# Degree count of a graph layer: the quotient one-hots stored with the chunk innermost, and one stair of every third group turned into a one-hot of VectorE

## The chip, the cores and the metric

One NeuronCore of one Trainium2 chip runs the kernel. The metric is the device time of one execution in microseconds (us), as the median of repeated runs.

## The reference

One layer of a graph network on 6,250 nodes of 512 features and 106,250 edges (50,000 drawn ones, both ways, and a loop for each node). Cut to what matters:

```
Q = relu(x @ Wq + bq);  V = x @ Wv + bv
deg  = segment_sum(ones, dst);  dinv = rsqrt(max(deg, 1e-12))
gcn  = segment_sum((x @ Wg)[src] * dinv[src] * dinv[dst], dst) + bg
out  = former(Q, V) + gcn + V          # cosine and sine sweeps over Q and V
out  = layernorm(x + relu(layernorm(out)))
```

The change lies in how `deg` is counted. Nothing else of the result is touched.

## The kernel before

The nodes are taken as 49 tiles of 128. The edges are sorted by `dst` and stand as 831 **chunks** of 128, one chunk in a column (a partition for each edge). The kernel has a first phase, in which for each tile t `x` is turned, multiplied by Wg and kept (`g_tile`), and a long second phase that gathers rows of `x @ Wg`, runs the sweeps and writes the output. The program of each engine is written out in order by hand, and the engines meet at semaphores.

The degree count rides on the first 31 tiles of the first phase (`HIST_TILES`). Each of these tiles does three **groups** b = 3t, 3t+1, 3t+2 of nine chunks (93 groups in all). `dst` is split into the remainder by 128 (`dst_mod`, the node in its tile) and the quotient (`dst_div`, the tile). For a group there are two operands in SBUF, each with two buffers that alternate:

- `div_hot`, the **quotient one-hots**: for each of the nine chunks 49 columns, 1 where the column's number is the edge's quotient. One VectorE instruction makes all 9 x 49 = 441 elements (L980), from the row 0..48 of `iota_bf`, read again for each chunk, and `dst_div`, of which one element is read 49 times.
- `mod_hot`, nine **wide hots** of 128 columns: for the first five chunks (`HOTS`) VectorE compares `iota_bf` with the remainder (a one-hot, L984, five instructions); for the last four (`STAIRS`) ScalarE takes the sign of column number plus 0.5 minus remainder (a stair of -1 and +1, L638, four instructions).

TensorE then multiplies, for each chunk, the wide hot by the quotient one-hots and adds into bank 5 (L1443, nine matmuls of 49 columns a group): one-hots into columns 0..48, stairs into columns 64..112. After tile 30 the stairs' sums are turned into counts by one small matmul.

The order of work in a tile t of the first 31:

- TensorE: wait for x's lower part of tile t; turn x of tile t+2 (L1428, four transposes); half of the product with Wg (L1382 to L1384, six matmuls of 512 columns); group 3t; the other half; groups 3t+1 and 3t+2.
- ScalarE: stairs of group 3t; copy turned x of t+2 from PSUM (L617, `g_step`); stairs of 3t+1 and 3t+2; copy the product of tile t (L621, `g_keep`); in tiles 0 to 7 one square of a kept tile (L626); in tiles 2 and 4 also a rounding of a weight (L602).
- VectorE: group 3t; lower part of x of tile t+2 (L993, `g_split`, waits for L617); groups 3t+1 and 3t+2; then what `between_tiles` puts there: a piece of a weight in odd tiles from 3 to 17 (L917), edge columns at tiles 6 and 8, limits of the tiles from 27 on.
- GpSimd fills constants at the start (`iota_bf` and others) and is idle until the second phase.

TensorE's group waits for VectorE (`bins_ready`) and ScalarE (`stairs_ready`); both wait for TensorE's group b-2 before they write into its buffer (`bins_used`).

Of the kernel before, what the change touches and what calls it, by code (L numbers as in the profile page):

```python
# [9 lines left out]
BF16 = mybir.dt.bfloat16  # L10
# [3 lines left out]
ALU = mybir.AluOpType  # L14
# [3 lines left out]
P = 128  # L18
# [12 lines left out]
def done(n):  # L31
    return n + (1 + LEAD)


def freed(n, depth):
    return n + (1 + LEAD - depth)


def build_layer(nc, x, src, dst, Wq, bq, Wv, bv, Wg, bg, gamma, beta, out):
# [3 lines left out]
    TILES = -(-N // P)  # L43
# [4 lines left out]
    GROUP, STAIRS = 9, 4  # L48
    HOTS = GROUP - STAIRS
# [5 lines left out]
    PAIRS = 4  # L55
# [30 lines left out]
    with ctx:  # L86
        def sb(name, shape, dt):
            return ctx.enter_context(nc.sbuf_tensor(name, shape, dt))
# [4 lines left out]
        def bank(name):  # L93
            return ctx.enter_context(nc.psum_tensor(name, [P, D], F32))
# [7 lines left out]
        pairs = sb("pairs", [P, PAIRS, PAIR], F32)  # L102
        with nc.sbuf_tensor("operands_f16", [P, 8, 2 * D], F16) as operands_f16:
# [40 lines left out]
        banks = [bank(f"bank{n}") for n in range(8)]  # L144
# [31 lines left out]
        dst_div = extra_row[:, :].bitcast(BF16)[:, 0:COLS]  # L176
# [3 lines left out]
        mod_hot = [hot_room[:, h * GROUP * 64:(h + 1) * GROUP * 64].bitcast(BF16).rearrange("p (c j) -> p c j", j=P)  # L180
                   for h in range(2)]
        DIVW = TILES + 1
        div_base = 2 * GROUP * 64
        div_hot = [hot_room[:, div_base + h * GROUP * DIVW // 2:div_base + (h + 1) * GROUP * DIVW // 2]
                   .bitcast(BF16).rearrange("p (c j) -> p c j", j=DIVW) for h in range(2)]
        iota_bf = sb("iota_bf", [P, P], BF16)
        zero_bf = sb("zero_bf", [P, P], BF16)
        UNIT_AT, STAIR_AT = 0, 64
# [46 lines left out]
        def column(ap, c):  # L235
            return ap[:, c:c + 1] if isinstance(c, int) else ap[:, bass.ds(c, 1)]
# [266 lines left out]
        def _(pool):  # L503
# [7 lines left out]
                               pattern=[[-1, P]], channel_multiplier=1).then_inc(s["consts_set"], 1)  # L511
            pool.iota(node_id[:, :], pattern=[[1, P]], base=0, channel_multiplier=0,
                      allow_small_or_imprecise_dtypes=True)
            pool.iota(iota_bf[:, :], pattern=[[1, P]], base=0, channel_multiplier=0,
                      allow_small_or_imprecise_dtypes=True)
            pool.iota(chunk_id, pattern=[[P, GROUPS]], base=0, channel_multiplier=1,
                      allow_small_or_imprecise_dtypes=True)
            pool.iota(first_node[:, :], pattern=[[P, TILES]], base=0, channel_multiplier=0,
                      allow_small_or_imprecise_dtypes=True)
# [8 lines left out]
                               pattern=[[-1, P]], channel_multiplier=1).then_inc(s["undo_ready"], 1)  # L528
            pool.wait_ge(s["undo_ready"], 2)
            pool.affine_select(out=undo, in_=undo, compare_op=ALU.not_equal, fill=-0.5, base=1,  # L530
                               pattern=[[-1, P]], channel_multiplier=1).then_inc(s["undo_ready"], 1)
            pool.wait_ge(s["undo_ready"], 3)
            pool.affine_select(out=undo[:, 0:1], in_=undo[:, 0:1], compare_op=ALU.not_equal, fill=0.5, base=1 - P,
                               pattern=[[-1, 1]], channel_multiplier=1).then_inc(s["undo_ready"], 1)
# [59 lines left out]
        def _(act):  # L594
# [39 lines left out]

            def stairs(b):
                act.wait_ge(s["bins_used"], freed(b, 2))
                for n in range(STAIRS):
                    last = act.activation(mod_hot[b % 2][:, HOTS + n, :], iota_bf[:, :], ACT.Sign,  # L638
                                          bias=column(stair_edge, b * STAIRS + n))
                last.then_inc(s["stairs_ready"], 1)  # L640
# [48 lines left out]
            for t in range(0, TILES):  # L689
                if t == 0:  # L690
                    act.wait_ge(s["columns_ready"], 1)
                if t < HIST_TILES:
                    stairs(3 * t)
                if t + 2 < TILES:
                    g_step(t + 2, t % 2, rows_of(t + 2))
                if t < HIST_TILES:
                    stairs(3 * t + 1)
                    stairs(3 * t + 2)
# [125 lines left out]
        def _(dve):  # L824
# [151 lines left out]
            def bins(b):  # L976
                c0, half = b * GROUP, b % 2

                dve.wait_ge(s["bins_used"], freed(b, 2))
                dve.tensor_tensor(div_hot[half][:, :, 0:TILES],  # L980
                                  iota_bf[:, 0:TILES].unsqueeze(1).to_broadcast([P, GROUP, TILES]),
                                  dst_div[:, c0:c0 + GROUP].unsqueeze(2).to_broadcast([P, GROUP, TILES]), ALU.is_equal)
                for c in range(HOTS):
                    last = dve.tensor_scalar(mod_hot[half][:, c, :], iota_bf[:, :], column(dst_mod, c0 + c), None,  # L984
                                             ALU.is_equal)
                last.then_inc(s["bins_ready"], 1)
# [72 lines left out]
            for t in range(0, TILES):  # L1059
                if t < HIST_TILES:  # L1060
                    bins(3 * t)
                keep_beside_g(t)
                if t + 2 < TILES:
                    g_split(t + 2, t % 2, rows_of(t + 2))
                if t < HIST_TILES:
                    bins(3 * t + 1)
                    bins(3 * t + 2)
                beside_g(t)
                between_tiles(t)
# [63 lines left out]
            h = stage[:, 2, 0:TILES]  # L1133
# [237 lines left out]
        def _(pe):  # L1371
# [65 lines left out]
            def bins(b):  # L1437
                half = b % 2
                pe.wait_ge(s["bins_ready"], done(b))
                pe.wait_ge(s["stairs_ready"], done(b))  # L1440
                for c in range(GROUP):
                    at = UNIT_AT if c < HOTS else STAIR_AT
                    last = pe.matmul(banks[5][:, at:at + TILES], mod_hot[half][:, c, :], div_hot[half][:, c, 0:TILES],  # L1443
                                     start=False, stop=False, skip_group_check=True)
                last.then_inc(s["bins_used"], 1)

# [20 lines left out]
            def g_tile(t, n, r):  # L1467
                pe.wait_ge(s["g_x_split"], done(t))
                if t + 2 < TILES:
                    g_turn(t + 2)  # L1470
                pe.wait_ge(s["g_kept"], freed(t, 2))
                g_product(t, n, r, [0, 1])
                if t < HIST_TILES:
                    bins(3 * t)
                g_product(t, n, r, [2, 3]).then_inc(s["g_summed"], 1)
                if t >= QV_TILES:
                    qv_beside_g(t)
                if t < HIST_TILES:
                    bins(3 * t + 1)
                    bins(3 * t + 2)  # L1480
                if t == HIST_TILES - 1:
                    pe.matmul(banks[5][:, 0:P], zero_bf[:, :], zero_bf[:, :], start=False, stop=True,
                              skip_group_check=True).then_inc(s["degrees_summed"], 1)
                between_tiles(t)
# [236 lines left out]
```

## Time and profile before

| what | value |
|---|---|
| runs of the kernel before | 1686.92 us median of 3 (1683.31 to 1688.21) |
| profiled execution | 1702.43 us, its span 1700.6 us |
| TensorE busy | 1529.1 us (90%) |
| VectorE busy | 1093.6 us (64%) |
| ScalarE busy | 608.9 us (36%) |
| GpSimd busy | 916.2 us (54%) |
| first and last quotient one-hots (L980) | start at 21.7 and 186.4 us |

The shares are means over the whole span. The degree count lies in its first 190 us; after that TensorE goes on with tiles 31 to 48 alone, and GpSimd's gathers begin at about 340 us. Starting times of an instruction are read as the pace of its engine, since the duration that the profile gives to one instruction overlaps with the next one's by some 80 ns on VectorE and ScalarE and more on TensorE.

### The profile page before, as it was taken

Reading aid. Unit: us, or ns where it says so; the run is one execution under the profiler, and the core shown is the slowest. Engines: PE = TensorE matmul, PEld = TensorE weight load, DVE = VectorE, ACT = ScalarE, POOL = GpSimd, SP = SyncE. Lnnn points to the kernel's source line nnn. Section 1 sums busy time; section 2 is a strip of 40 time slices with the busy share of each in tenths; the row PEclk is TensorE's granted clock in tenths of the full one; section 3 lists DMA queues with packets and bytes.
Section 4 is the critical chain, followed back from the end, with each engine's and each line's share of the span. In section 5 each row is a group of like instructions: output and inputs, shape, how many; then the busy total and the mean of one; then the engine's idle time right before and its main releaser. Section 6 shows DMA issues by size and latency. Waiting matters only on the chain.

```text
span 1700.6 us, 25340 instructions
## 1 busy us (share of the span) xinstructions
PE 1529.1 (90%) x7913; PEld 943.0 (55%) x7913; DVE 1093.6 (64%) x3318; ACT 608.9 (36%) x1384; POOL 916.2 (54%) x1026
## 2 busy tenths in 40 slices
PE   5788999899999997999998999889999999999994
PEld 3566777666555563443433433336666766666663
DVE  6999676676666666434445444447777768777774
ACT  5999875533233222111112111113333333333332
POOL 0000000166666766666676777666666666666662
PEclk9999999999999997999999999989999999999997
DMA  6444444598888888888888888879888888888884
GB/s 224 139 154 160 151 157 153 201 314 291 297 285 286 290 287 263 262 266 267 266 253 257 264 270 273 271 208 288 283 271 279 277 271 277 286 273 271 285 256 142
DMA packets 172759, 423.89 MB, mean 249 GB/s; under 512 B 24142, under 2 KB 25802, under 8 KB 172616
## 3 DMA queue, kind: packets, MB, share of 16 engines
q0 software_dynamic: 71120, 236.74, 45.5%
q1 hardware_dynamic: 79980, 146.16, 25.1%
q10 hardware_dynamic: 21516, 39.29, 6.1%
q8 instruction: 65, 1.06, 0.2%
q14 instruction: 78, 0.64, 0.1%
HBM read 351.42 MB, written 70.67 MB: 248 GB/s over the span
## 4 chain that ended last, share of the span: by engine, by line
PE 60%; issue 12%; DVE 10%; DMA 7%; POOL 4%; ACT 4%; another core or an unknown queue 1%; POOLq 0%; SPq 0%; DVEq 0%; ACTq 0%
PE bank L1382 13%; PE bank L1383 12%; PE bank L1384 12%; PE bank L1503 10%; PE bank L1505 9%; POOL gathered L566 4%; DMA gathered<-scaled_g,index_slots 3%; DVE stage L984 3%; DVE stage L980 2%; ACT stage L638 1%; DMA scaled_g<-pairs 1%; DVE operands L993 1%; ACT operands L617 1%; DMA combine<-values 1%
## 5 line engine op out<-in xcount | busy, mean ns | idle before, releaser
L566 POOL DMA_INDIRECT gathered<-scaled_g,index_slots x882 | 877.1, 994 | 418.1 <-issue 203.8
L1100 DVE TENSOR_SCALAR one_hot<-iota_bf,dst_in_tile,gathered 128x128 bf16<-128x128 bf16 x882 | 269.7, 327 | 373.8 <-DMA gathered<-scaled_g,index_slots 212.9
L1503 PE MATMUL bank<-gathered,one_hot 128*128 128x512 f16 x882 | 344.9, 391 | 77.0 <-issue 39.4
L1382 PE MATMUL bank<-weights,operands 128*128 128x512 f32 x784 | 398.4, 508 | 14.2 <-DVE stage L1000 4.4
L1505 PE MATMUL bank<-gathered,one_hot 128*128 128x512 f16 x882 | 339.6, 385 | 5.1 <-issue 4.6
L1383 PE MATMUL bank<-weights,operands 128*128 128x512 f32 x784 | 313.7, 400 | 1.8 <-issue 1.8
L1384 PE MATMUL bank<-weights,operands 128*128 128x512 f32 x784 | 312.6, 399 | 0.6 <-issue 0.6
L1503 PEld LDWEIGHTS bank<-gathered,one_hot 128*128 128x128 bf16 x882 | 85.5, 97 | 253.5 <-issue 163.5
L736 ACT ACTIVATE operands_f<-operands,cos_sin_v 128x512 f16<-128x512 f32 x98 | 70.2, 721 | 360.5 <-remote 171.2
L1382 PEld LDWEIGHTS bank<-weights,operands 128*128 128x128 f32 x784 | 150.7, 192 | 80.7 <-issue 7.6
L551 POOL COPY dst_slots<-dst_cols 128x18 f32 x49 | 12.7, 260 | 332.7 <-issue 331.2
L1384 PEld LDWEIGHTS bank<-weights,operands 128*128 128x128 f32 x784 | 149.4, 191 | 38.9 <-issue 2.3
L1383 PEld LDWEIGHTS bank<-weights,operands 128*128 128x128 f32 x784 | 150.8, 192 | 26.2 <-issue 3.9
L755 ACT ACTIVATE operands<-stage,stats 128x512 fp32r<-128x512 f32 x98 | 70.9, 723 | 228.4 <-issue 121.0
L1384 PE MATMUL bank<-operands_f,nodes 128*128 128x512 f16 x392 | 149.1, 380 | 3.9 <-issue 3.9
L1382 PE MATMUL bank<-operands_f,nodes 128*128 128x512 f16 x392 | 149.3, 381 | 1.3 <-issue 1.3
L1383 PE MATMUL bank<-operands_f,nodes 128*128 128x512 f16 x392 | 149.3, 381 | 0.5 <-issue 0.3
L638 ACT ACTIVATE stage<-iota_bf,combine 128x128 bf16<-128x128 bf16 x372 | 115.8, 391 | 8.1 <-DVE combine L873 6.3
L1505 PEld LDWEIGHTS bank<-gathered,one_hot 128*128 128x128 bf16 x882 | 87.7, 99 | 43.2 <-issue 7.5
L1382 PE MATMUL bank<-gathered,operands 128*128 128x512 f32 (+1 forms) x196 | 85.0, 434 | 0.0
L984 DVE TENSOR_SCALAR stage<-iota_bf,nodes 128x128 bf16<-128x128 bf16 x465 | 83.5, 247 | 0.0
L1189 DVE SCALAR_TENSOR_TENSOR operands_f<-operands,cos_sin_v,operands_f 128x512 f16<-128x512 f32 x98 | 73.0, 746 | 14.2 <-ACT operands_f L736 8.8
(243 smaller groups left out, 2066.8 us busy)
## 6 DMA issues: line engine op xcount, KB each, us to landing
operands<-values SPq DMA_DIRECT2D x98, 256.0 KB
stage<-in_x SPq DMA_DIRECT2D x96, 256.0 KB, 2.7
turned_x<-operands SPq DMA_DIRECT2D x37, 512.0 KB, 3.3
operands<-turned_x SPq DMA_DIRECT2D x37, 512.0 KB
gathered<-scaled_g,index_slots POOLq DMA_INDIRECT x882
scaled_g<-pairs SPq DMA_DIRECT2D x49, 260.0 KB, 2.0
pairs<-scaled_g SPq DMA_DIRECT2D x49, 260.0 KB
values<-stage ACTq DMA_DIRECT2D x49, 256.0 KB
```

Source lines behind the costliest of these rows:

```text
L566: pool.indirect_dma_start(out=plain(row_ring[k % RING]), out_offset=None, in_=table, in_offset=bass.IndirectOffsetOnAxis(ap=index_slots[:, ...
L638: last = act.activation(mod_hot[b % 2][:, HOTS + n, :], iota_bf[:, :], ACT.Sign, bias=column(stair_edge, b * STAIRS + n))
L736: act.activation(v_hi, m_values(g), ACT.Copy, scale=column(cos_sin_v, g % TILES * 2 + g // TILES))\
L755: act.activation(operands[:, 5 + n % 2, :], stage[:, 2 + j, :], ACT.Square, bias=st[:, 1:2], accum_out=st[:, 2:3]).then_inc(s[f"o_squared{ ...
L984: last = dve.tensor_scalar(mod_hot[half][:, c, :], iota_bf[:, :], column(dst_mod, c0 + c), None, ALU.is_equal)
L1100: dve.tensor_scalar(one_hot[:, k % HOT, :], iota_bf[:, :], column(dst_in_tile, seq % 2 * PER_TILE + k), scale_of(row), ALU.is_equal, ALU.m ...
L1189: dve.scalar_tensor_tensor(v_lo, m_values(g), column(cos_sin_v, g % TILES * 2 + g // TILES), v_hi, ALU.mult, ALU.subtract).then_inc(s["m_s ...
L1382: pe.matmul(out_ap, a_hi, b_hi, start=start and n == 0, stop=False, skip_group_check=True)
L1383: pe.matmul(out_ap, a_hi, b_lo, start=False, stop=False, skip_group_check=True)
L1384: last = pe.matmul(out_ap, a_lo, b_hi, start=False, stop=stop and n == len(pairs) - 1, skip_group_check=True)
L1503: pe.matmul(gcn_banks[seq % 2][:, :], one_hot[:, k % HOT, :], hi, start=k == 0, stop=False, skip_group_check=True)
L1505: pe.matmul(gcn_banks[seq % 2][:, :], one_hot[:, k % HOT, :], lo, start=False, stop=False, skip_group_check=True).then_inc(s["chunk_summed ...
```

## The change

The nine quotient one-hots of a group are stored with the chunk innermost: element (quotient j, chunk c) at 9j + c, where it was at 50c + j. VectorE makes them in one instruction as before; its first operand is now a new constant, `counter`, in which each number 0..49 stands nine times in a row (450 elements, made by GpSimd at the start, in room of `pairs` that is not used until much later), and its second is the row of the group's nine quotients, read again for each j. All three operands are 2 bytes wide and have a step of one element. TensorE reads the 49 columns of a chunk with a step of nine elements, 18 bytes, where it read them next to each other.

In each third group of a tile (b % 3 == 2) VectorE makes six wide one-hots instead of five, and ScalarE three stairs instead of four.

```
-                   .bitcast(BF16).rearrange("p (c j) -> p c j", j=DIVW) for h in range(2)]
+                   .bitcast(BF16).rearrange("p (j c) -> p j c", c=GROUP) for h in range(2)]
+        counter = pairs[:, PAIRS - 1, 0:GROUP * DIVW // 2].bitcast(BF16).rearrange("p (j c) -> p j c", c=GROUP)
+
+        def hots_of(b):
+            return HOTS + (b % 3 == 2)
...
+            pool.iota(counter, pattern=[[1, DIVW], [0, GROUP]], base=0, channel_multiplier=0,
+                      allow_small_or_imprecise_dtypes=True)
...
-                for n in range(STAIRS):
+                for n in range(hots_of(b) - HOTS, STAIRS):
...
-                dve.tensor_tensor(div_hot[half][:, :, 0:TILES],
-                                  iota_bf[:, 0:TILES].unsqueeze(1).to_broadcast([P, GROUP, TILES]),
-                                  dst_div[:, c0:c0 + GROUP].unsqueeze(2).to_broadcast([P, GROUP, TILES]), ALU.is_equal)
-                for c in range(HOTS):
+                dve.tensor_tensor(div_hot[half][:, 0:TILES, :], counter[:, 0:TILES, :],
+                                  dst_div[:, c0:c0 + GROUP].unsqueeze(1).to_broadcast([P, TILES, GROUP]), ALU.is_equal)
+                for c in range(hots_of(b)):
...
-                    at = UNIT_AT if c < HOTS else STAIR_AT
-                    last = pe.matmul(banks[5][:, at:at + TILES], mod_hot[half][:, c, :], div_hot[half][:, c, 0:TILES],
+                    at = UNIT_AT if c < hots_of(b) else STAIR_AT
+                    last = pe.matmul(banks[5][:, at:at + TILES], mod_hot[half][:, c, :], div_hot[half][:, 0:TILES, c],
```

On VectorE the instructions of tile 2 stand as follows in the program before (`stage` holds both kinds of hots, `extra_row` the quotients; the first row is the last of group 6):

```order
L984 TENSOR_SCALAR stage<-iota_bf,nodes 128x128 x5
L993 TENSOR_TENSOR operands<-bank1,operands 128x512
L980 TENSOR_TENSOR stage<-iota_bf,extra_row 128x9x49
L984 TENSOR_SCALAR stage<-iota_bf,nodes 128x128 x5
L980 TENSOR_TENSOR stage<-iota_bf,extra_row 128x9x49
L984 TENSOR_SCALAR stage<-iota_bf,nodes 128x128 x5
```

and so in the changed program, where line numbers are six or seven higher (`pairs` holds the counter):

```order
L990 TENSOR_SCALAR stage<-iota_bf,nodes 128x128 x5
L999 TENSOR_TENSOR operands<-bank1,operands 128x512
L987 TENSOR_TENSOR stage<-pairs,extra_row 128x441
L990 TENSOR_SCALAR stage<-iota_bf,nodes 128x128 x5
L987 TENSOR_TENSOR stage<-pairs,extra_row 128x441
L990 TENSOR_SCALAR stage<-iota_bf,nodes 128x128 x6
```

The order is the same; the quotient compare runs as one row of 441 elements instead of nine rows of 49, and the third group has one more wide one-hot.

On ScalarE a tile of the count without a square stands so before (L617 and L621 are the two copies from PSUM):

```order
L638 ACTIVATE stage<-iota_bf,combine 128x128 x4
L617 CAST operands<-bank 128x512
L638 ACTIVATE stage<-iota_bf,combine 128x128 x8
L621 COPY nodes<-bank 128x512
L638 ACTIVATE stage<-iota_bf,combine 128x128 x4
```

and so after the change:

```order
L645 ACTIVATE stage<-iota_bf,combine 128x128 x4
L624 CAST operands<-bank 128x512
L645 ACTIVATE stage<-iota_bf,combine 128x128 x7
L628 COPY nodes<-bank 128x512
L645 ACTIVATE stage<-iota_bf,combine 128x128 x4
```

The stair that is gone is one of the eight between the two copies.

## Rows read from the trace of the kernel before

**Rows 1.** Busy time of each engine in stretches (start and end in us).

```profile
core 0: us, PE busy (x) PEld busy (x) DVE busy (x) ACT busy (x) POOL busy (x), PEclk, DMA share, GB/s
32.00:64.00 32.00, 22.78 (x235) 16.73 (x234) 27.42 (x110) 31.81 (x90) 0.00 (x0) 1.00 0.41 141
88.00:190.00 102.00, 85.78 (x861) 64.64 (x858) 98.20 (x382) 92.03 (x274) 0.00 (x0) 1.00 0.43 150
```

**Rows 2.** Timeline of VectorE, one tile; columns: start, duration, instruction, idle before.

```profile
142.84 0.69 DVE L993 TENSOR_TENSOR operands<-bank,operands 128x512 fp32r<-128x512 f32 x1 [0.25 <-ACT operands L617]
143.45 0.61 DVE L980 TENSOR_TENSOR stage<-iota_bf,extra_row 128x441 bf16<-128x441 bf16 x1
...
144.79 0.61 DVE L980 TENSOR_TENSOR stage<-iota_bf,extra_row 128x441 bf16<-128x441 bf16 x1
...
147.80 0.69 DVE L993 TENSOR_TENSOR operands<-bank,operands 128x512 fp32r<-128x512 f32 x1 [0.25 <-ACT operands L617]
```

**Rows 3.** Timeline of TensorE in the tile behind it.

```profile
146.27 0.40 PE L1443 MATMUL bank<-stage 128*128 128x49 bf16 x9 [0.71 <-DVE stage L984]
146.51 0.63 PE L1428 MATMUL bank<-ident,stage 128*128 128x128 f32 x4
...
150.12 0.40 PE L1443 MATMUL bank<-stage 128*128 128x49 bf16 x9
```

**Rows 4.** Timeline of ScalarE there.

```profile
145.35 0.59 ACT L621 COPY nodes<-bank 128x512 f32<-128x512 f32 x1 [0.20 <-PE bank L1384]
145.84 1.27 ACT L638 ACTIVATE stage<-iota_bf,combine 128x128 bf16<-128x128 bf16 x4
147.18 0.59 ACT L617 CAST operands<-bank 128x512 fp32r<-128x512 f32 x1
...
150.31 0.59 ACT L621 COPY nodes<-bank 128x512 f32<-128x512 f32 x1 [0.20 <-PE bank L1384]
```

**Rows 5.** Timeline of ScalarE, tiles 5 and 6.

```profile
54.97 2.45 ACT L638 ACTIVATE stage<-iota_bf,combine 128x128 bf16<-128x128 bf16 x8
57.32 0.57 ACT L621 COPY nodes<-bank 128x512 f32<-128x512 f32 x1
57.92 0.63 ACT L626 ACTIVATE squares_out<-nodes 128x512 bf16<-128x512 f32 x1
...
62.59 0.59 ACT L621 COPY nodes<-bank 128x512 f32<-128x512 f32 x1
```

**Rows 6.** Timeline of VectorE: L993 in the lists of tiles 9, 19, 27, 29, 30.

```profile
77.03 0.68 DVE L993 TENSOR_TENSOR operands<-bank,operands 128x512 fp32r<-128x512 f32 x1
...
127.95 0.69 DVE L993 TENSOR_TENSOR operands<-bank,operands 128x512 fp32r<-128x512 f32 x1 [0.25 <-ACT operands L617]
...
167.66 0.69 DVE L993 TENSOR_TENSOR operands<-bank,operands 128x512 fp32r<-128x512 f32 x1 [0.25 <-ACT operands L617]
...
178.69 0.68 DVE L993 TENSOR_TENSOR operands<-bank,operands 128x512 fp32r<-128x512 f32 x1
...
184.43 0.68 DVE L993 TENSOR_TENSOR operands<-bank,operands 128x512 fp32r<-128x512 f32 x1
```

**Rows 7.** Groups of VectorE by line and shape, 0 to 200 us.

```profile
L980 DVE TENSOR_TENSOR stage<-iota_bf,extra_row 128x441 bf16<-128x441 bf16 x93 | 57.0, 613 | 1.4 <-PE bank L1443 1.3
...
L939 DVE TENSOR_TENSOR nodes<-nodes 128x896 f32<-128x896 f32 x1 | 1.1, 1082 | 0.0
...
L937 DVE TENSOR_SCALAR nodes<-nodes 128x896 f32<-128x896 f32 x1 | 0.6, 616 | 0.0
```

**Rows 8.** Timeline of TensorE in tile 0, at its slower pace.

```profile
24.82 0.60 PE L1443 MATMUL bank<-stage 128*128 128x49 bf16 x9
25.24 0.78 PE L1382 MATMUL bank<-gathered,operands 128*128 128x512 f32 x1
```

**Rows 9.** Timeline at the start.

```profile
2.68 0.18 POOL L518 IOTA first_node<- 128x49 f32 x1
...
4.79 0.63 DVE L856 CAST nodes<-nodes 128x896 f32<-128x896 int32 x1 [1.53 <-DMA nodes<-in_dst]
```

## The prediction

> **What bounds the kernel now.** The change lies in the first 190 us, so I first read the busy times by stretch, not the page's shares. Between 32 and 64 us ScalarE is busy 31.8 of 32 us; between 88 and 190 us VectorE is busy 98.2 of 102 us, with ScalarE at 92.0 and TensorE at 85.8 [rows 1]. No engine is far behind: what an edit frees on one meets the next soon. So I read the three timelines of one tile and follow who releases whom. (Starts of instructions give the pace; I call L993 of a tile the start of its lap on VectorE.)
>
> The **short loop**, tiles 19 to 26: L993 starts at 142.84, two groups follow, and TensorE's last group of the tile starts at 146.27, having waited 0.71 us for VectorE: 3.43 us [rows 2, 3]. TensorE needs 0.24 us for the nine matmuls, then turns x (146.51); ScalarE's copy L617 starts at 147.18 and the next L993 at 147.80, having waited 0.25 us for that copy [rows 2 to 4]. 3.43 + 0.24 + 0.67 + 0.62 = 4.96 us, the pace of these tiles. The group ahead of L993 is outside this loop (its cover is the 0.25 us).
>
> The **long loop** takes two tiles: TensorE from its last group (146.27) through turn, product, group and product until ScalarE's L621 starts at 150.31, 4.04 us [rows 3, 4]; L621 0.49; four stairs; L617 0.62 until L993; and VectorE's 3.43. The stairs stand 1.34 us long there (145.84 to 147.18), but eight of them in a row take 57.32 - 54.97 = 2.35 us, 0.294 each [rows 4, 5], so four need 1.17. Sum 9.75, or 4.88 a tile: only 0.08 below the short one.
>
> In tiles 1 to 7 ScalarE's own list is as tight. From L621 to L621 is 5.27 us with a square [rows 5]; twelve stairs (3.53), L621 (0.60 until the square starts) and the square with its tail (0.63) leave 0.51 for L617, about what a copy takes, so the engine has hardly a gap. And the long loop with a square (57.92 less the copy: 0.73) is 10.48, 5.24 a tile. VectorE's own list is 0.61 + 3 x 1.34 = 4.64 us a tile [rows 2]; in the odd tiles from 9 to 17 it has L917 as well, of the same shape as L993 (0.6), and is full. L993 goes from 77.03 to 127.95 in ten tiles, 10.18 a pair, so 5.22 in the odd ones and 4.96 in the even [rows 6]. Tiles 28 and 29 have a long extra each and take 5.74 (178.69 to 184.43) [rows 6].
>
> **What each edit costs.** *The compare.* 441 elements take 613 ns. The same kind of instruction on 896 elements takes 1082, so an element costs 469/455 = 1.03 ns, one a clock; L937, which reads one tensor, takes 616 for 896, 466 less, which is two elements a clock [rows 7]. No row has a two-tensor instruction on 2-byte operands with a step of one throughout. Bounds: nothing, or half of 441 x 1.03 = 0.23 us saved. I take 0.23: before, one operand repeats an element innermost, after the change all three run through neighbours, and the nearest row, L937, shows the engine at two a clock once it has the room. The Trainium skill (Vector Engine (DVE) Microarchitecture Reference, 5.1 Performance modes) states that two-tensor instructions run two elements a cycle when all are 2 bytes with an innermost step of one and more than one element, and that one element read repeatedly keeps them at one. It makes the same sum, and the 613 ns of before agree with its second half.
>
> *The sixth one-hot.* 1.34 us a group (143.45 to 144.79) less the compare's 0.53 leaves 0.81 for five, so 0.16 each on VectorE [rows 2]. In the stretch L993 to TensorE's last group both groups save 0.23 and the second gains 0.16: 0.30 less. VectorE's whole lap loses 3 x 0.23 - 0.16 = 0.53. *The third stair.* ScalarE's lap loses 0.29, all of it between L617 and L621, thus in neither loop; it counts only where ScalarE's list is the bound.
>
> *The strided read.* 837 matmuls read 49 elements 18 bytes apart. They start 0.24/9 = 27 ns apart now [rows 3]. No row has such a read. Below, nothing. Above, the nearest row is the same nine matmuls at TensorE's slower pace in tile 0: 25.24 - 24.82 = 0.42, 47 ns each, 20 more [rows 8]. I take 16 more, near that end, since the clock is granted in full there [rows 1], 49 columns at 2.4 GHz are 20.4 ns of the 27, and a column that costs two clocks makes 41 to 47. That is 0.144 us a group. It falls into the short loop once and the long loop twice, and half of what VectorE gave goes back. By the Trainium skill (Advanced Engine Details and Errata, SBUF Cachelines) a line is 16 bytes, and full speed wants two hits on one; 18 bytes never hit twice, so the rule speaks against this edit, but gives no figure. By the rule unheeded the sum is 9.9; with my value it is 6.6.
>
> *The counter.* An IOTA of 49 elements takes 0.18 us [rows 9]; 450 make under 1.7 at that rate even with nothing fixed, in front of what VectorE's constants wait for. VectorE waits there 1.53 us for the edges [rows 9] and later for a weight, so I cost it at nothing; without that cover it would be up to 1.7.
>
> **The sum.** New short loop 4.96 - 0.30 + 0.144 = 4.80; new long loop 9.75 - 0.30 + 0.288 = 9.74 for two tiles, 4.87; with a square 10.47.
> - Tiles 1 to 5: ScalarE's list is the bound (two weights are rounded there): 5 x 0.29 = 1.46. Tiles 6, 7: the long loop with a square hardly moves (10.48 to 10.47), so they add nothing; less 0.1 for tile 0's groups: 1.4.
> - Tiles 8 and 9: the first also turns the source columns and follows the short loop, 0.16; the second is VectorE's whole lap, 0.53: 0.7.
> - Tiles 9 to 18, five pairs after that: 10.18 becomes 9.74: 5 x 0.44 = 2.2.
> - Eight laps from 127.95 to 167.66 [rows 6]: 4.96 becomes 4.87: 0.75.
> - Tiles 27 to 30, VectorE's lap: 0.41, 0.53, 0.53, then 0.30 less 0.14 for the last: 1.6.
>
> Together 6.6 us. Behind the count TensorE is the bound and was waiting for its last group, so what it gains moves everything after it. The profiled execution would go from 1702.4 to 1695.8, and the median from 1686.9 to **1680.3**, 0.39% less; the profiled execution stands 15.5 us above the median, and I take the same gain off both. A measurement of this kernel can tell about 0.3%, 5.1 us, from no change.
>
> **Rivals.**
> - *The read is free.* Loops 4.66 and 9.45: tiles 1 to 7 1.8, tiles 8 and 9 0.8, five pairs 3.65, eight laps 1.9, the last 1.8: 9.9; 1677.0. For it: a matmul has 6.6 ns over its columns' time now, room in which a slower read could begin. Against: no row reads with a gap, so nothing shows it. 22%.
> - *TensorE becomes the bound, slower than before.* TensorE's own lap is 150.12 + 0.24 - 146.27 = 4.09 [rows 3]. Each ns on a matmul takes 0.009 us from each of some 25 tiles, 0.225 us; my 6.6 at 16 ns are gone at 45 ns more, that is 72 ns or more than three clocks a column. At 50 more its lap is 4.09 + 27 x 0.050 = 5.44 against 5.11 on average between 77.03 and 184.43 in 21 tiles [rows 6]: 7 us lost, with three tiles before them 7.5, less 1.4 of the first five: +6, 1693. 12%.
> - *The compare doesn't speed up* (rows of nine, starts at odd elements). Then the sixth one-hot is a loss: short loop 5.27, pairs 10.65, whole laps +0.16. +2.3 (five pairs), +2.4 (eight laps), +0.8 (last), +0.5 (8, 9), -1.0 (first): +5, 1692. 8%.
> - *The gain does not arrive*: it is given back behind the count, where TensorE's granted clock falls in places or a queue is late: 1687. 8%.
> - My forecast: 50%.
>
> **The numbers.** Faster by over 0.3%: three quarters of the forecast (the bound is 1.5 us away, and three runs spread by 4.9), nearly all of the free read: 0.58. Slower: half to two thirds of the second and third rival and little more: 0.14. Same: 0.28. Range 1674.5 to 1690: below, the free read with 2.5 us of spread; above, no gain with as much; it leaves out most of the two slow rivals. The likeliest one's own range is 1677 to 1684.
>
> **What would show it.** The compare at 0.38 us instead of 0.61. Nine matmuls 0.39 apart instead of 0.24; 0.24 would be the free read, over 0.6 the slow one. L993's step in tiles 19 to 26 at 4.87 (4.73 free; 5.4 slow). Seven stairs between L617 and L621, the sixth one-hot on VectorE. L993 in tile 30's list starting at 177.9 instead of 184.43 [rows 6], and everything behind it earlier by the same, unless it is given back. I am wrong most easily by the size of the read, since both loops cross TensorE's groups. ScalarE's list, 5.2 less the square and less 0.29, is 4.3 and sets no floor above the forecast's 4.87.

## The result: slower by 1.1%, and the profile after

The changed kernel takes 1706.83 us (median of 4, 1700.32 to 1708.93) against 1686.96 (4 runs). The ratio is 1.0108, 95% interval 1.0085 to 1.0131: slower by 18 us, more than the 0.3% that can be told from no change. I had forecast 1680.3 in a range to 1690.

The busy times in the stretches of [rows 1], now of the changed kernel:

```profile
core 0: us, PE busy (x) PEld busy (x) DVE busy (x) ACT busy (x) POOL busy (x), PEclk, DMA share, GB/s
32.00:64.00 32.00, 30.52 (x224) 24.88 (x223) 24.72 (x111) 29.63 (x80) 0.00 (x0) 1.00 0.40 140
88.00:190.00 102.00, 102.00 (x766) 85.95 (x765) 80.17 (x359) 81.71 (x233) 0.00 (x0) 1.00 0.39 135
```

TensorE is busy without a gap from 88 to 190 us, where it had 16 us of idle time, though it did 95 instructions fewer there (766 against 861). VectorE went from 98.2 to 80.2. The bound has moved to TensorE.

One tile on TensorE (start, duration, instruction; L1449 is the count's matmul, L1434 the turn of x):

```profile
144.85 1.82 PE L1449 MATMUL bank<-stage 128*128 128x49 bf16 x18
146.49 0.62 PE L1434 MATMUL bank<-ident,stage 128*128 128x128 f32 x4
...
148.35 0.99 PE L1449 MATMUL bank<-stage 128*128 128x49 bf16 x9
149.12 0.48 PE L1388 MATMUL bank<-gathered,operands 128*128 128x512 f32 x1
...
150.60 1.82 PE L1449 MATMUL bank<-stage 128*128 128x49 bf16 x18
152.24 0.62 PE L1434 MATMUL bank<-ident,stage 128*128 128x128 f32 x4
```

Eighteen matmuls take 152.24 - 150.60 = 1.64 us, 91 ns each, where nine took 0.24 us, 27 each [rows 3]. The lap is 5.75 us (146.49 to 152.24) instead of 4.96. Both other engines now wait for TensorE to free their buffers (VectorE and ScalarE in that tile):

```profile
151.62 0.42 DVE L987 TENSOR_TENSOR stage<-pairs,extra_row 128x441 bf16<-128x441 bf16 x1 [0.73 <-PE bank L1449]
```

```profile
149.38 0.99 ACT L645 ACTIVATE stage<-iota_bf,combine 128x128 bf16<-128x128 bf16 x3 [0.47 <-PE bank L1449]
```

The compare itself did get faster, 411 ns against 613 [rows 7]:

```profile
L987 DVE TENSOR_TENSOR stage<-pairs,extra_row 128x441 bf16<-128x441 bf16 x93 | 38.2, 411 | 13.8 <-PE bank L1449 13.1
```

Where the count ends is seen in the one matmul that closes its sums. First the kernel before, then the changed one (minimum, median and maximum duration, first and last start):

```profile
L1482 PE MATMUL bank<-zero_bf x1: 216/216/216, 188.1 to 188.1; 128*128 128x128 bf16 x1
```

```profile
L1488 PE MATMUL bank<-zero_bf x1: 242/242/242, 204.0 to 204.0; 128*128 128x128 bf16 x1
```

15.9 us later, and GpSimd's first gather is later by 15.5 (349.0 against 333.5). The loss is made in the count and arrives whole at the second phase. The two profiled executions differ by only 4.8 us (1707.23 against 1702.43), because the one of before happened to stand 15.5 us above its own median; so one profile against the other would have hidden three quarters of the loss. I therefore compare the count's own length in the traces, and times by the ratio of runs on one chip.

### The profile page after: what moved, and what is told of

Read it like the earlier page. It is cut to its first block, busy times and chain, and to the rows that moved or that the text cites. A ratio compares the mean times of both kernels' runs of the same rounds, so it can differ in the third digit from the quotient of the medians.

```text
span 1705.0 us, 25341 instructions
## 1 busy us (share of the span) xinstructions
PE 1568.5 (92%) x7913; PEld 989.2 (58%) x7913; DVE 1086.2 (64%) x3349; ACT 605.8 (36%) x1353; POOL 911.5 (53%) x1027
## 4 chain that ended last, share of the span: by engine, by line
PE 70%; DMA 8%; issue 8%; DVE 6%; ACT 3%; POOL 3%; another core or an unknown queue 1%; POOLq 0%; SPq 0%; ACTq 0%; DVEq 0%
PE bank L1388 14%; PE bank L1389 14%; PE bank L1390 14%; PE bank L1509 10%; PE bank L1511 9%; DMA gathered<-scaled_g,index_slots 5%; PE bank L1449 4%; POOL gathered L573 2%; DMA scaled_g<-pairs 2%; PE bank L1434 1%; PE bank L1640 1%; ACT pairs L639 1%; DMA combine<-values 1%; DVE one_hot L1106 1%
## 5 line engine op out<-in xcount | busy, mean ns | idle before, releaser
L1106 DVE TENSOR_SCALAR one_hot<-iota_bf,dst_in_tile,gathered 128x128 bf16<-128x128 bf16 x882 | 273.3, 329 | 378.0 <-DMA gathered<-scaled_g,index_slots 203.2
L645 ACT ACTIVATE stage<-iota_bf,combine 128x128 bf16<-128x128 bf16 x341 | 109.5, 391 | 25.6 <-PE bank L1449 19.3
L1449 PE MATMUL bank<-stage 128*128 128x49 bf16 x837 | 87.3, 271 | 1.5 <-ACT stage L645 0.9
L990 DVE TENSOR_SCALAR stage<-iota_bf,nodes 128x128 bf16<-128x128 bf16 x496 | 88.4, 247 | 0.0
```

What stands on the lines that cost most here:

```text
L1106: dve.tensor_scalar(one_hot[:, k % HOT, :], iota_bf[:, :], column(dst_in_tile, seq % 2 * PER_TILE + k), scale_of(row), ALU.is_equal, ALU.m ...
```

## The experiments

Eight of the ten stand in one table; e4 and e8, in which TensorE's read changes from tile to tile, ran once each and are read by tile below. The count's length runs from the matmul that clears its sums to the one that closes them (in the kernel before 16.8 to 188.1); the last column is the ratio times the time of before on that chip. The four kernels e5 to e8 ran on a chip on which the kernel before takes 1592.9 us; elsewhere it takes 1686.6 (e1 to e4) and 1688.1 (e9, e10). All lengths are set against the one trace that there is of the kernel before.

| kernel | count's length, us | against before | time by ratio (95%) | us |
|---|---|---|---|---|
| before | 171.3 | | 1 | |
| changed | 187.4 | +16.1 | 1.0108 (1.0085 to 1.0131) | +18.2 |
| e1 read alone | 188.5 | +17.2 | 1.0101 (1.0078 to 1.0124) | +17.0 |
| e2 all but the read | 162.3 | -9.0 | 0.9942 (0.9923 to 0.9962) | -9.8 |
| e3 sixth one-hot alone | 177.0 | +5.7 | 1.0022 (1.0008 to 1.0036) | +3.7 |
| e5 pairs | 169.2 | -2.1 | 0.9980 (0.9968 to 0.9992) | -3.2 |
| e6 threes | 166.3 | -5.0 | 0.9964 (0.9950 to 0.9978) | -5.7 |
| e7 pairs, split by tile | 165.0 | -6.3 | 0.9964 (0.9949 to 0.9980) | -5.7 |
| e9 even pairs | 162.0 | -9.3 | 0.9949 (0.9930 to 0.9967) | -8.6 |
| e10 even pairs, split by tile | 159.7 | -11.6 | 0.9928 (0.9902 to 0.9953) | -12.2 |

The change of the count's length and that of the time agree within the intervals in every row: the rest of the program only shifts.

### e1: the strided read alone

```
 (the kernel before)
-                    last = pe.matmul(..., div_hot[half][:, c, 0:TILES],
+                    last = pe.matmul(..., stepped[half][:, 0:TILES, c],      # same buffer, viewed as (j c), step 9
```

(This kernel, e4 and e8 also set the two buffers to zero once at the start.)

> The kernel before, with one edit: TensorE reads the 49 columns of a chunk with a step of nine elements in the same buffer. The compare on VectorE, its layout and the split of wide hots stay, so the counts are of other elements. Theory A, the read alone makes the matmul slow: nine matmuls stand 0.77 to 0.82 us apart as in the changed kernel, TensorE's lap is 5.75 us in tiles 19 to 26, and the time is 1702 to 1710 us, about the changed kernel's. Theory B, the matmul is slow because VectorE's faster compare writes the same part of SBUF at two elements a clock while TensorE reads: here they stay near 0.24 to 0.4 us and the time stays within 5 us of 1687.

Measured: 1705.49 us, ratio 1.0101. TensorE of this kernel (L1446 is the count's matmul):

```profile
146.40 1.82 PE L1446 MATMUL bank<-stage 128*128 128x49 bf16 x18
148.03 0.62 PE L1431 MATMUL bank<-ident,stage 128*128 128x128 f32 x4
```

1.63 us for 18, 91 ns each, with VectorE's compare as slow as before (615 ns). Theory A holds and B falls: VectorE's faster writes are not needed for it.

### e2: everything but the strided read

```
 (the changed kernel)
-                    last = pe.matmul(..., div_hot[half][:, 0:TILES, c],
+                    last = pe.matmul(..., packed[half][:, c, 0:TILES],       # same buffer, 49 neighbours
```

> The changed kernel, with one edit: TensorE reads 49 neighbouring elements for each chunk, so the counts are of other elements; the faster compare, the counter, the sixth one-hot and the third stair stay. Theory A: nine matmuls 0.24 us apart, L993's step in tiles 19 to 26 at 4.73 us, pairs with the weight piece 9.45, 9.9 us less than before, 1677 us. Theory B: the matmuls stay slow, about 1700 us. Theory C, part of the loss comes from behind the count and not from the read: the count ends 9.9 us earlier but the time is not below 1685.

Measured: 1679.28 us, ratio 0.9942. Its VectorE, two laps:

```profile
140.81 0.69 DVE L1001 TENSOR_TENSOR operands<-bank,operands 128x512 fp32r<-128x512 f32 x1 [0.46 <-ACT operands L626]
...
145.59 0.69 DVE L1001 TENSOR_TENSOR operands<-bank,operands 128x512 fp32r<-128x512 f32 x1 [0.51 <-ACT operands L626]
...
150.32 0.69 DVE L1001 TENSOR_TENSOR operands<-bank,operands 128x512 fp32r<-128x512 f32 x1 [0.47 <-ACT operands L626]
```

The laps alternate 4.78 and 4.73 us, 9.51 for two where the long loop was to give 9.45, and the count is 9.0 us shorter where I had 9.9. The parts came each a tenth or so short of their forecast (L993 against L1001: tiles 1 to 9 gain 2.4 where 2.6 was forecast, the five pairs 3.3 for 3.65, the eight laps 1.7 for 1.9, the last 1.6 for 1.8), so the terms of the sum other than the read were right together, and not by errors that cancel. Theory C falls: what the count gains, the time gains.

### e3: the sixth one-hot alone

```
 (the kernel before)
-                for n in range(STAIRS):
+                for n in range(hots_of(b) - HOTS, STAIRS):
-                for c in range(HOTS):
+                for c in range(hots_of(b)):
```

> The kernel before, with only the sixth one-hot and the missing stair of each third group; compare and read as before. By the loops VectorE's 0.16 us lands in the short loop: L993's step in tiles 19 to 26 5.12 us, pairs with the weight piece 10.5, the first five tiles 0.29 us less each: together 2 us more, 1689. Rival: if ScalarE is what limits the whole count, 31 x 0.29 = 9 us less, 1678.

Measured: 1690.76 us, ratio 1.0022, slower. The laps on VectorE are as worked out:

```profile
141.75 0.69 DVE L996 TENSOR_TENSOR operands<-bank,operands 128x512 fp32r<-128x512 f32 x1 [0.25 <-ACT operands L620]
...
146.88 0.69 DVE L996 TENSOR_TENSOR operands<-bank,operands 128x512 fp32r<-128x512 f32 x1 [0.25 <-ACT operands L620]
```

5.13 us against 5.12, and the rival (ScalarE limits the whole count) falls. But the count is 5.7 us longer, not 2. From tile 9 on it loses 3.5 us, as the loops gave (1.6, 1.3 and 0.5). The excess lies before, where TensorE's clock was granted in part in two places, in stretches of this kernel:

```profile
45.00:49.50 4.50, 4.34 (x30) 3.39 (x31) 4.29 (x16) 2.96 (x10) 0.00 (x0) 0.62 0.35 102
54.00:58.50 4.50, 2.28 (x24) 1.58 (x24) 3.53 (x15) 4.47 (x15) 0.00 (x0) 1.00 0.30 117
58.50:63.00 4.50, 4.44 (x30) 3.46 (x31) 4.29 (x15) 3.05 (x11) 0.00 (x0) 0.62 0.39 122
```

From 45 to 49.5 us and from 58.5 to 63 us it was granted 0.62, a mix of the two levels; in the kernel before it was 1.00 in both stretches. The step of L996 that holds the first is 7.88 us (47.08 to 54.97), where the one of the same kind two laps earlier took 6.45; the one that holds the second is 6.81 us (60.36 to 67.17), against 5.39 for the lap ahead of it (5.27 and 5.23 in the kernel before). That is 1.4 us each, 2.8 of the 3.7 that the count is longer than forecast. TensorE had waited 0.23, 0.58 and 1.10 us for the other engines before the first and 1.39, 0.57 and 1.10 before the second; the kernel before waits 0.94, 0.57 or 0.56, and 0.94 in the same places, so why its clock stayed is not shown. The profiled execution of e3 is also the longest of its twelve (1698.01 us).

### e4: the price of a column against its distance

```
 (the kernel before; step = 1 + tile % 9)
-                    last = pe.matmul(..., div_hot[half][:, c, 0:TILES],
+                    last = pe.matmul(..., flat[half][:, 0:(TILES - 1) * step + 1:step],
```

> The kernel before with TensorE's step through the quotient one-hots set by the tile: step 1, 2, ... 9 elements (2 to 18 bytes) in tiles 0 to 8, then again; the counts are of other elements. It shows the price of a column against its distance. Theory A1, a 16-byte line: near 27 ns a matmul up to 8 bytes of step, rising between, and 91 ns at 18 bytes. Theory A2, any gap breaks a paired read of neighbours: 91 ns or a fixed higher price from step 2 on. Theory A3, only steps over 16 bytes cost: 27 ns to step 8, 91 at step 9.

TensorE, the last group of tiles 1, 2, 4, 7 and 8 with what starts behind it (steps of 2, 3, 5, 8 and 9 elements):

```profile
33.19 0.40 PE L1446 MATMUL bank<-stage 128*128 128x49 bf16 x9 [0.94 <-DVE stage L987]
33.43 0.64 PE L1431 MATMUL bank<-ident,stage 128*128 128x128 f32 x4
...
38.42 0.50 PE L1446 MATMUL bank<-stage 128*128 128x49 bf16 x9 [0.79 <-DVE stage L987]
38.75 0.63 PE L1431 MATMUL bank<-ident,stage 128*128 128x128 f32 x4
...
50.65 0.68 PE L1446 MATMUL bank<-stage 128*128 128x49 bf16 x9 [0.28 <-DVE stage L987]
51.15 0.62 PE L1431 MATMUL bank<-ident,stage 128*128 128x128 f32 x4
...
69.08 0.97 PE L1446 MATMUL bank<-stage 128*128 128x49 bf16 x9 [0.17 <-DVE stage L987]
69.87 0.95 PE L1396 MATMUL bank<-ident,nodes 128*128 128x128 f32 x7
...
74.76 1.82 PE L1446 MATMUL bank<-stage 128*128 128x49 bf16 x18
76.39 0.62 PE L1431 MATMUL bank<-ident,stage 128*128 128x128 f32 x4
```

The distance of the two starts, by nine (by 18 for the steps 7 and 9), gives:

| step, elements (bytes) | 1 (2) | 2 (4) | 3 (6) | 4 (8) | 5 (10) | 6 (12) | 7 (14) | 8 (16) | 9 (18) |
|---|---|---|---|---|---|---|---|---|---|
| ns a matmul | 27 | 27 | 37 | 46 | 56 | 67 | 78 | 88 | 91 |
| 16-byte lines in 49 columns | 7 | 13 | 19 | 25 | 31 | 37 | 43 | 49 | 49 |

From step 3 to 8 each element of step adds 10 ns, and six lines: 1.7 ns a line, about four clocks at 2.4 GHz. (These distances take in the first matmul of a group, behind which the second comes later than the others at step 1 (39 ns) and sooner at step 9 (some 70). Between the later ones the trace's single records stand 25, 25, 37, 47, 58, 69, 79, 90 and 92 ns apart, which makes a line 1.8 ns; that it is four clocks exactly is not shown.) Up to a step of two (13 lines, 22 ns) the 27 ns that the matmul takes anyway hide it; from 16 bytes on each column has a line to itself and the price stays. A1 comes nearest, but its corner was put too far out: I had expected 27 ns up to 8 bytes of step, and 46 was measured. A2 and A3 fall.

### e8: columns at a fixed step

```
 (the kernel before; step and wide by tile % 6)
-                    last = pe.matmul(banks[5][:, at:at + TILES], ..., div_hot[half][:, c, 0:TILES],
+                    last = pe.matmul(banks[5][:, at:at + wide], ..., flat[half][:, 0:(wide - 1) * step + 1:step],
```

> The kernel before with step and number of columns of TensorE's matmuls set by the tile, in turn (step, columns) = (1, 49), (9, 49), (9, 32), (9, 16), (1, 16), (5, 49); the counts are of other elements and not all columns are summed. If each column at 18 bytes costs four clocks, 1.67 ns, the 49, 32 and 16 columns stand 91, 62 and 36 ns apart; if the price is a fixed one for a read with a gap, all stand near 91. (1, 16) shows the floor of a matmul, 27 ns or less.

Last groups with steps of 9 elements over 49 columns, 9 over 16, and 1 over 16:

```profile
32.33 0.99 PE L1447 MATMUL bank<-stage 128*128 128x49 bf16 x9 [0.36 <-DVE stage L987]
33.14 0.62 PE L1431 MATMUL bank<-ident,stage 128*128 128x128 f32 x4
...
45.14 0.46 PE L1447 MATMUL bank<-stage 128*128 128x16 bf16 x9 [0.88 <-DVE stage L987]
45.44 0.64 PE L1431 MATMUL bank<-ident,stage 128*128 128x128 f32 x4
...
50.37 0.38 PE L1447 MATMUL bank<-stage 128*128 128x16 bf16 x9 [0.95 <-DVE stage L987]
50.61 0.64 PE L1431 MATMUL bank<-ident,stage 128*128 128x128 f32 x4
```

90, 33 and 27 ns a matmul (32 columns: 57): the price goes with the columns, 57 ns for the 33 between 16 and 49, 1.7 each, and is not one of having a gap. Sixteen neighbouring columns take the same 27 ns as forty-nine did [rows 3]: the 6.6 ns that I had read as overhead over the columns' time belong to a floor; what sets it is not shown.

### e5 and e6: the same compare with a short step for TensorE

Two or three chunks innermost, in five or three blocks:

```
 (the changed kernel, e5; e6 with 3 for 2 and three blocks)
-                dve.tensor_tensor(div_hot[half][:, 0:TILES, :], counter[:, 0:TILES, :],
-                                  dst_div[:, c0:c0 + GROUP].unsqueeze(1).to_broadcast([P, TILES, GROUP]), ALU.is_equal)
+                dve.tensor_tensor(div_hot[half][:, :, 0:TILES, :],
+                                  counter[:, 0:TILES, :].unsqueeze(1).to_broadcast([P, BLOCKS, TILES, 2]),
+                                  dst_div[:, c0:c0 + 2 * BLOCKS].rearrange("p (a c) -> p a c", c=2).unsqueeze(2)
+                                  .to_broadcast([P, BLOCKS, TILES, 2]), ALU.is_equal)
```

> The changed kernel with the quotient one-hots stored in five blocks of two chunks (the tenth chunk is never read), chunk innermost in its block, the counter with each number twice; the compare is one instruction over 5 x 49 x 2 = 490 elements, all with a step of one, and TensorE's step is two elements, 4 bytes. In the step sweep a step of two cost nothing (27 ns a matmul). Theory A (TensorE pays for 16-byte lines, each worth four columns of time): matmuls 27 ns apart, compare 0.43 to 0.44 us, L993's step in tiles 19 to 26 at 4.75 us, time as with the changed kernel but its read, 1679 us. Theory B (in a real two-element row the compare falls back to one element a clock): compare 0.66 us, lap 5.2 us, 1693 us.

> The changed kernel with three blocks of three chunks, chunk innermost in its block: TensorE's step is three elements, 6 bytes. Theory A: matmuls 37 ns apart as at step three of the sweep (10 more), compare 0.41 us, L993's step in tiles 19 to 26 at 4.82 us against 4.73 to 4.78 with a free read, time 1681 us. If the sweep's price was an accident of its place, 27 or 91 ns.

Measured: ratios 0.9980 and 0.9964, both faster than before, but e5, whose read is free, less than e6. VectorE of e5 shows why:

```profile
140.63 0.66 DVE L988 TENSOR_TENSOR stage<-pairs,extra_row 128x490 bf16<-128x490 bf16 x1
...
142.02 0.41 DVE L988 TENSOR_TENSOR stage<-pairs,extra_row 128x490 bf16<-128x490 bf16 x1
...
143.32 0.66 DVE L988 TENSOR_TENSOR stage<-pairs,extra_row 128x490 bf16<-128x490 bf16 x1
```

and the minimum, median and maximum of e6's compare:

```profile
L987 DVE TENSOR_TENSOR stage<-pairs,extra_row x93: 456/466/481, 20.9 to 180.5; 128x441 bf16<-128x441 bf16 x93
```

Every second compare of e5 takes 0.66 us: group b starts at element 9b of the quotients, at an odd one in every second group. So its laps in tiles 19 to 26 are 4.97, no shorter than before. Theories A and B were each half right: TensorE's nine matmuls do take 0.24 us (27 each), and in e6 0.33 (37 each), as swept; e6's laps are 4.90 and not 4.82, since its compare takes 0.466 us where I had put 0.41. All compares fit one rule (D): the clocks are the 4-byte words that each row of the quotients touches. A row of nine touches five words from any start, 49 x 5 = 245; a row of two one or, from an odd start, two: 5 x 49 = 245 or 490; a row of three always two, 3 x 49 x 2 = 294. With 1.04 ns a clock and 0.15 us more: 0.41, 0.41, 0.66, 0.46 us, against 0.411, 0.41, 0.66 and 0.466 measured. The rule is drawn from these row lengths alone.

### e9: pairs that start even

```
 (e5; dst_div with ten places for each group's nine)
+            link(dve.tensor_copy(dst_div.rearrange("p (b c) -> p b c", c=GROUP + 1)[:, :, 0:GROUP],
+                                 div_i[:, 0:3 * HIST_TILES * GROUP].rearrange("p (b c) -> p b c", c=GROUP)))
```

> The kernel with pairs, but the quotients of a group now start at an even element (ten places for a group's nine, so that each pair lies in one 4-byte word). Theory D (the compare's clocks are the 4-byte words that the rows of its second operand touch): every compare 0.41 us, where those of odd groups took 0.66; L993's step in tiles 19 to 26 4.75 us, the last group of the count 9 us earlier than in the kernel before, time 0.6% below it. Rival: the 0.66 us belongs to one of the two buffers and not to the start of the quotients; then nothing changes, 0.2% below.

Its compares, all 93:

```profile
L990 DVE TENSOR_TENSOR stage<-pairs,extra_row x93: 398/405/418, 21.2 to 176.1; 128x490 bf16<-128x490 bf16 x93
```

None slow, with the same two buffers in turn, so the rival falls and D stands. Laps of 4.72 and 4.78, the count 9.3 us shorter, ratio 0.9949: what the change could have been.

### e7 and e10: the sixth one-hot only where ScalarE is the bound

```
-            return HOTS + (b % 3 == 2)
+            return HOTS + (b % 3 == 2 and b < 24)
```

> As the kernel with pairs, but the sixth one-hot and the missing stair only in the first eight tiles, where ScalarE also squares and rounds; from tile 8 on five one-hots and four stairs as before. By the loops VectorE's 0.16 us leaves the short loop: steps in tiles 19 to 26 4.65 us (the long loop, 9.29 for two), pairs with the weight piece 9.3, last laps 0.16 less: 2 us less than with pairs, 1677 us. Rival: ScalarE's twelve stairs become the bound there, 4.75 or more, and nothing is won.

> The same with even starts, and the sixth one-hot only in the first eight tiles. Theory D: compare 0.41 us, step in tiles 19 to 26 4.65 to 4.7 us (the long loop and ScalarE's twelve stairs, 4.6 with its two copies), 11 us earlier than the kernel before at the count's end, time 0.7% below. Rival: ScalarE or TensorE's lap holds the step at 4.75 or more; then no better than with the sixth one-hot throughout.

e7 carries the slow odd starts: its step is 4.81 us (141.76 to 146.57), not 4.65, and its time is no better than that of e6 (the same ratio, the count 1.3 us shorter). Against e5, which differs in nothing else, its count is 4.2 us shorter where 2 were forecast. e10 reaches the forecast, two laps of it on VectorE:

```profile
138.74 0.69 DVE L1004 TENSOR_TENSOR operands<-bank,operands 128x512 fp32r<-128x512 f32 x1 [0.61 <-ACT operands L625]
...
143.36 0.69 DVE L1004 TENSOR_TENSOR operands<-bank,operands 128x512 fp32r<-128x512 f32 x1 [0.52 <-ACT operands L625]
...
148.09 0.69 DVE L1004 TENSOR_TENSOR operands<-bank,operands 128x512 fp32r<-128x512 f32 x1 [0.63 <-ACT operands L625]
```

4.62 and 4.73, 9.35 for two. ScalarE goes from one instruction to the next there with hardly a gap, and VectorE waits for its copy by over 0.5 us a lap, so ScalarE is the next bound by this trace; no run tests it. The ratio is 0.9928, 12 us below the kernel before: the best version here, though its interval (0.9902 to 0.9953) overlaps that of e9.

## Why the prediction was wrong

**The loops: right.** Short and long loop gave 4.73 without the read's cost (e2: 4.73 and 4.78) and 5.12 with the sixth one-hot alone (e3: 5.13). VectorE's, ScalarE's and the counter's terms summed to 9.9 us; e2 gained 9.0 in its count and 9.8 in its time. A gain there did move everything behind it.

**The compare: right in kind, 0.20 us and not 0.23.** 411 ns, since a row of nine costs five ticks and not four and a half.

**The strided read: the step that failed.** It says "I take 16 more, near that end", and ahead of it "Above, the nearest row is the same nine matmuls at TensorE's slower pace in tile 0 ... 20 more". Measured: 64 more. The row named as the upper bound showed what a column costs at half the clock, and nothing about a read; that a column could cost more than two clocks was not excluded by any row, and I used the row as though it were. 64 ns on 27 matmuls is 1.73 us a tile; TensorE's own lap of 4.09 becomes 5.8 (5.75 measured), above both loops, so every other term of the sum is hidden under it: e1, without the faster compare, is as slow as the whole change.

**The rival.** "TensorE becomes the bound" had the mechanism and its place, at 12%. Its turning point was put too far out: 45 ns more is where the loops alone would have given the gain back, but by the same rows TensorE's lap grows by 0.027 us for each ns and the loops by 0.009, so it overtakes them (4.09 + 0.027 d against 4.73 + 0.009 d) at 35 ns more and reaches the average lap of before, 5.11, at 38. It was priced at 50 ns, +6 us and 1693; at 64 ns TensorE's lap holds in nearly every tile: thirty laps of 5.75 are 173 us, and with 12 us from the clearing matmul (16.6) to the end of tile 0 (28.6) they make 185 of the 187 us that the count took; three of the first seven laps have more in them (6.81, 6.81 and 6.53) and bring the rest. In those seven laps the change loses only 1.0 us against before; 14 of the 16.1 are lost from tile 8 on, where every lap is 5.75. The rival's chance was low for the same reason that its price was: no row bore it out, and none bore the 16 ns out either. The range should have reached to where the unknown cost ended, and I had no end for it.

**The rule that spoke against the change.** The Trainium skill (Advanced Engine Details and Errata, SBUF Cachelines) says a line is 16 bytes and full speed wants at least two hits on it. The traces agree on the 16 bytes (the price stops growing there) and differ on the hits: at 8 bytes of step, two columns a line, a matmul took 46 ns and not 27; at 4 bytes, four columns a line, it took 27. The other page used (Vector Engine (DVE) Microarchitecture Reference, 5.1 Performance modes) was right that the mode engages. It also says that with two sources a pair may span two rows and that 4-byte alignment makes no difference. For a second source that repeats a short row, e5, e6 and e9 show otherwise.

## What to carry to other kernels

A layout that makes one engine's write or compare fast must be priced at its reader as well: in these bf16 matmuls the moving operand costs about four of TensorE's clocks (1.7 ns) for each 16-byte line it touches, so for 2-byte data keep at least four columns in a line (a step of at most 4 bytes); longer steps grow in price until 16 bytes. The two wishes could be met together here: two items innermost, starting on a 4-byte word, were enough for VectorE's packed pace (0.41 us) and free for TensorE (27 ns a matmul) in e9. And an unknown price needs an end that bounds that very mechanism; where no row has it, the range must take in the point at which the costed engine would become the bound and beyond.

## What the runs showed of the hardware that was not expected

- TensorE reads one 16-byte line of the moving operand in about four clocks of 2.4 GHz (1.7 ns): 37, 46, 56, 67, 78, 88 ns for 49 columns at steps of 3 to 8 elements, 91 at 9, and 33 for 16 columns at 9.
- A bf16 matmul behind a bf16 weight load stands no closer than 27 ns to the next (mean of nine): 49 or 16 neighbouring columns take the same.
- VectorE's packed compare takes a clock for each 4-byte word of a repeated row: rows of two took 0.41 us from even starts and 0.66 from odd ones, over 490 elements.
- In e3 TensorE's granted clock fell to 0.62 in two stretches of 4.5 us, each time behind three waits of at most 1.39 us within some 5 us, and each time one lap became 1.4 us longer. The kernel before, with waits of 0.94, 0.57 and 0.94 us in the same places, kept 1.00.
